# Expert loops with four row buffers and loads three quads ahead, unrolled by four; last combine's sum into X on VectorE

## The reference, cut to what matters

```python
x = x + _L0_ffn_ref(_layernorm(x), ...)   # 16 experts, top 2, silu(x w1) * (x w2), then w3, hidden 256
x = x + _L1_ffn_ref(_layernorm(x), ...)   # 8 experts, top 1 with a capacity, relu(x w1 + b1) w2 + b2, hidden 512
x = x + _L3_ffn_ref(_layernorm(x), ...)   # 64 x 192 tokens' attention first, then 8 experts, top 2, hidden 341
# of L3, the end:
for e in range(NE):
    hh = silu(flat @ w1[e].T) * (flat @ w3[e].T)
    out = out + weights[:, e:e+1] * (hh @ w2[e].T)
return x + out.reshape(Bx, Tx, Cx)
```

## Time and profile before

| | |
|---|---|
| median of 3 runs | 3395.41 us (3390.82 to 3404.48) |
| the profiled execution's own time | 3369.56 us |
| its span, first to last instruction | 3367.8 us |
| mean granted TensorE clock | 0.912 |
| busy: PE, DVE, ACT, POOL | 2731.9, 2195.4, 1751.4, 872.8 us |

### The profile page before, as it was taken

One profiled execution on the slowest core, in us unless ns is written; L12 is line 12 of the kernel. 1 busy time (PEld: TensorE's weight loads), 2 busy tenths in 40 slices (PEclk: granted clock), 3 DMA queues, 4 the chain that ended last, 5 costly groups with the idle time before them and its releaser, 6 DMA issues. The chain is left out here.

```text
span 3367.8 us, 68105 instructions
## 1 busy us (share of the span) xinstructions
PE 2731.9 (81%) x19770; PEld 2142.4 (64%) x19770; DVE 2195.4 (65%) x6539; ACT 1751.4 (52%) x5050; POOL 872.8 (26%) x863
## 2 busy tenths in 40 slices
PE   5799995787777686578999997899978777569995
PEld 4566674777467575366787776566655445468883
DVE  5666674444567554668888885799986677544443
ACT  2233332444466353465656563677757666445554
POOL 0222333444425333330010001000001434434331
PEclk9899997989878798889999999899999888689998
DMA  5111111222332111320000000000010000022125
GB/s 194 43 51 43 57 45 50 63 63 63 125 123 74 50 51 54 135 66 1 1 0 0 0 1 22 14 25 19 25 59 8 25 20 21 27 57 56 53 55 162
DMA packets 142570, 168.85 MB, mean 50 GB/s; under 512 B 19920, under 2 KB 118224, under 8 KB 141776
## 3 DMA queue, kind: packets, MB, share of 16 engines
q1 hardware_dynamic: 116688, 118.67, 11.9%
q0 software_dynamic: 21504, 44.74, 3.9%
q10 hardware_dynamic: 4224, 3.59, 0.4%
HBM read 115.87 MB, written 51.05 MB: 50 GB/s over the span
## 5 line engine op out<-in xcount | busy, mean ns | idle before, releaser
L1363 PE MATMUL bank<-ffn_e_xT,ffn_e_mine 128*128 128x128 f32 x3360 | 454.7, 284 | 27.3 <-ACT ffn_e_mine L1297 11.7
L1221 POOL DMA_INDIRECT y_rows<-ffn_e_rows_out,ffn_e_scatter_at x352 | 339.1, 963 | 522.4 <-DVE ffn_e_rows_out L1249 331.1
L1363 PEld LDWEIGHTS bank<-ffn_e_xT,ffn_e_mine 128*128 128x128 f32 x3360 | 421.8, 199 | 35.4 <-issue 30.0
L744 POOL DMA_INDIRECT sorted_rows<-ffn_rows,ffn_slot x320 | 315.9, 987 | 229.7 <-issue 218.3
L1269 DVE TENSOR_TENSOR ffn_e_hid<-ffn_e_act,bank 128x256 f32<-128x256 f32 (+1 forms) x280 | 135.9, 485 | 274.1 <-ACT ffn_e_act L1323 214.8
L1373 PE MATMUL bank<-ffn_e_mine,ffn_e_hid 128*128 128x128 f32 x1968 | 292.0, 283 | 9.0 <-issue 5.0
L1297 ACT ACTIVATE ffn_e_mine<-constants 128x512 f32 (+1 forms) x352 | 250.4, 712 | 93.3 <-issue 80.6
L1373 PEld LDWEIGHTS bank<-ffn_e_mine,ffn_e_hid 128*128 128x128 f32 x1968 | 258.1, 197 | 15.3 <-issue 6.6
L2736 ACT ACTIVATE gnn_prob<-bank,gnn_low 128x256 f32<-128x256 f32 x512 | 203.1, 500 | 108.0 <-DVE gnn_low L2650 108.0
L1323 ACT ACTIVATE ffn_e_act<-bank 128x256 f32<-128x256 f32 (+1 forms) x280 | 120.5, 430 | 244.1 <-PE bank L1363 199.3
L1257 DVE TENSOR_SCALAR ffn_e_mine<-constants 128x256 f32 (+2 forms) x352 | 124.0, 354 | 131.1 <-PE bank L1373 68.1
(11 more groups left out here) (514 smaller groups left out, 6558.3 us busy)
## 6 DMA issues: line engine op xcount, KB each, us to landing
g_adj<-in_adjT SPq DMA_DIRECT2D x48, 512.0 KB, 3.8
ffn_e_rows_in<-sorted_rows SPq DMA_DIRECT2D x346, 66.0 KB
ffn_c_y<-y_rows SPq DMA_DIRECT2D x80, 256.0 KB, 3.1
g_adj_rows<-in_adj SPq DMA_DIRECT2D x16, 512.0 KB
gnn_adj<-in_adjT SPq DMA_DIRECT2D x16, 512.0 KB, 3.9
constants<-in_ffn SPq DMA_DIRECT2D x1, 6281.0 KB, 23.0
y_rows<-ffn_e_rows_out,ffn_e_scatter_at POOLq DMA_INDIRECT x352
constants<-in_ffn SPq DMA_DIRECT2D x1, 5204.0 KB, 15.4
```

What stands on the lines that cost most here:

```text
L744: eng.indirect_dma_start(c.sorted_rows, bass.IndirectOffsetOnAxis(r.slot[par][:, k, j:j + 1], 0), r.rows[par][:, j, :], None).then_inc(r.d ...
L1221: g.indirect_dma_start(c.y_rows, bass.IndirectOffsetOnAxis(scatter_at[par][:, k:k + 1], 0), rows_out[par][:, k, :], None).then_inc(scatter ...
L1363: ins = pe.matmul(chunk(part, ch), chunk(weights[:, i * HALF:(i + 1) * HALF], ch), x, start=True, stop=True)
```

## The change

In `moe_experts`, `rows_in` has four buffers for two, and the semaphores of their loads four for two. The load of quad q waits for the transposes and the token columns of quad q-4 where it waited for those of quad q-2. The loops of SP, DVE, ACT and PE go through a new `by_fours`: four quads written out, a loop whose body is four quads (7, 3 and 7 times round), and the last two or four quads written out. POOL's loop stays.

In the last `moe_combine` alone, PE does nothing and ACT's copies back to `X` are gone. DVE, after its weighed sum of a turn, waits for it and adds it to `X`, and counts up `rows_ready`. SP waits for that alone.

```diff
+def by_fours(eng, body, count=TURNS):
+    stop = 4 + 4 * ((count - 5) // 4)
+    for t in range(4):
+        body(t, t, t == 0, False)
+    with eng.Fori(4, stop - 3, 4) as t:
+        for i in range(4):
+            body(t + i, i, False, False)
+    for t in range(stop, count):
+        body(t, t % 4, False, t == count - 1)
...
-        rows_in = [sb(f"rows_in{i}", [P, Q, ROW]) for i in range(2)]
+        rows_in = [sb(f"rows_in{i}", [P, Q, ROW]) for i in range(4)]
...
-                    wait_past(sp, xT_ps, q - 1)
-                    wait_past(sp, token_ready, q - 1)
+                    wait_past(sp, xT_ps, q - 3)
+                    wait_past(sp, token_ready, q - 3)
                     for k, at in zip(mine, places):
-                        sp.dma_start(rows_in[par][:, k, :], c.sorted_rows[ds(at, P), :]).then_inc(gathered[par], 16)
-                every_turn(sp, load, QUADS)
+                        sp.dma_start(rows_in[four][:, k, :], c.sorted_rows[ds(at, P), :]).then_inc(gathered[four], 16)
+                by_fours(sp, load, QUADS)
...
-                every_turn(v, quad, QUADS)
+                by_fours(v, quad, QUADS)
...
-                every_turn(a, quad, QUADS)
+                by_fours(a, lambda q, four, first, last: quad(q, four % 2, first, last), QUADS)
...
-                    pe.wait_ge(gathered[par], 8 * Q * (q - par) + 16 * Q)
+                    pe.wait_ge(gathered[four], 4 * Q * (q - four) + 16 * Q)
...
-                every_turn(pe, quad, QUADS)
+                by_fours(pe, quad, QUADS)
...
                     if t >= DEEP:
-                        sp.wait_ge(added_ps, t - DEEP + 1)
+                        sp.wait_ge(rows_ready if ends else added_ps, t - DEEP + 1)
                         if ends:
-                            sp.wait_ge(rows_ready, t - DEEP + 1)
                             store(t - DEEP)
...
                         ins.then_inc(summed, 1)
+                        if ends:
+                            v.wait_ge(summed, t + 1)
+                            rows_ = c.X[:, ds(t * TT, TT), :]
+                            v.tensor_tensor(rows_, rows_, acc[:], ALU.add).then_inc(rows_ready, 1)
...
-                for t in range(TURNS):
+                for t in range(0 if ends else TURNS):
                     par, bank = t % DEEP, B[t % 8][:]
...
-                    if t >= 2:
+                    if t >= 2 and not ends:
                         rows_out(t - 2)
-                rows_out(TURNS - 2)
-                rows_out(TURNS - 1)
+                for t in range(TURNS if ends else TURNS - 2, TURNS):
+                    rows_out(t)
```

More of the change, by code:

```diff
@@ L1165, in moe_experts @@
             "first_copied second_copied other_ready token_ready targets_set xT_ps xT_ready h_ps act_ready hid_ready y_ps y_ready").split())
-        gathered, scattered = ([c.dma_sem[name, n, i] for i in range(2)] for n in ("gathered", "scattered"))
+        gathered, scattered = ([c.dma_sem[name, n, i] for i in range(count)] for n, count in (("gathered", 4), ("scattered", 2)))
         def first_banks(k):
@@ L1200, in _, with load @@
             def _(sp):
-                def load(q, par, first, last):
+                def load(q, four, first, last):
                     mine = range(Q // 2) if first else range(Q)
@@ L1228, in _, with set_targets @@
             def _(v):
-                def set_targets(q, par):
-                    v.wait_ge(gathered[par], 8 * Q * (q - par) + 16 * Q)
+                def set_targets(q, four):
+                    v.wait_ge(gathered[four], 4 * Q * (q - four) + 16 * Q)
                     at = ds(q * Q, Q)
                     now = counted(v, q + 1)
-                    v.tensor_tensor(other[:], rows_in[par][:, :, D + 1], r.tile_order[:, at], ALU.not_equal).then_inc(other_ready, 1)
+                    v.tensor_tensor(other[:], rows_in[four][:, :, D + 1], r.tile_order[:, at], ALU.not_equal).then_inc(other_ready, 1)
                     v.wait_ge(other_ready, now)
-                    v.scalar_tensor_tensor(other[:], other[:], float(TOKENS), rows_in[par][:, :, D], ALU.mult, ALU.add).then_inc(token_ready, 1)
+                    v.scalar_tensor_tensor(other[:], other[:], float(TOKENS), rows_in[four][:, :, D], ALU.mult, ALU.add).then_inc(token_ready, 1)
                     v.wait_ge(token_ready, now)
@@ L1258, in copy_second, with quad @@
                                     ALU.mult).then_inc(second_copied, 1)
-                def quad(q, par, first, last):
+                def quad(q, four, first, last):
                     experts = quad_experts(v, q)
@@ L1278, in quad @@
                         if k == 0:
-                            set_targets(q, par)
+                            set_targets(q, four)
                         if k == 3 and not first:
-                            results(q - 1, 1 - par)
+                            results(q - 1, (four + 1) % 2)
                 for k, e in zip(range(AHEAD), quad_experts(v, 0)):
                     copy_second(k, e)
-                every_turn(v, quad, QUADS)
+                by_fours(v, quad, QUADS)
                 results(QUADS - 1, 1)
@@ L1376, in _, with quad @@
                 to_features(0, 0)
-                def quad(q, par, first, last):
+                def quad(q, four, first, last):
+                    par = four % 2
                     for k in range(Q):
@@ L1381, in quad @@
                         if k == 0 and not last:
-                            to_features(q + 1, 1 - par)
+                            to_features(q + 1, (four + 1) % 4)
                         if not (first and k < LAG):
                             second_product(*unit_before(q, par, k, LAG))
-                every_turn(pe, quad, QUADS)
+                by_fours(pe, quad, QUADS)
                 for k in range(LAG):
@@ L3384, in program @@
         c.bank = [ctx.enter_context(nc.psum_tensor(f"bank{i}", [P, 512], F32)) for i in range(8)]
-        c.dma_sem = {(name, n, i): c.sem(f"{name}_{n}{i}") for name in MOE for n in ("dispatched", "gathered", "scattered", "padded") for i in range({"padded": 1, "dispatched": 4}.get(n, 2))}
+        c.dma_sem = {(name, n, i): c.sem(f"{name}_{n}{i}") for name in MOE for n in ("dispatched", "gathered", "scattered", "padded") for i in range({"padded": 1, "scattered": 2}.get(n, 4))}
         c.w_ready = {n: c.sem("w_ready_" + n) for n in order}
```

4 lines of the change are left out of this document (2 added, 2 removed).

## The result

The changed kernel takes 3369.51 us (median of 4 runs, 3366.19 to 3378.20), the kernel before beside it 3399.05 us (4 runs, 3390.82 to 3404.48): a ratio of 0.9921, 95% interval 0.9901 to 0.9941. That is 29.5 us or 0.8% faster, about half of the 63 us that were forecast. The time lies in the range, which reached up to the rival in which the queue takes the gain back. So the two spans can't be subtracted. Stage by stage, the trace after is 11 us longer in the first graph layer, 5 us longer in the attention (neither is touched by the change), and 10.0 us shorter in the last combine.

The account below looks back on a forecast made before the run. PE was taken as the bound (81% busy), waiting for rows in ffn0, with SP's issuing next. Savings of 44 + 1 + 12 + 0 + 6 = 63 us from 3395.4 gave 3332 us, range 3288 to 3380.

Parts of the forecast that it names:

- the queue takes the gain back: Rival: bursts meet all four scatters, SP needs 8.0 us a quad in ffn0; 22 us saved, 3373 us, chance 0.15.
- rows 7: Profile rows in ffn0: first product through at 624.34, ACT's silu only at 627.52, when the load burst ends.
- Rows earlier, ffn0: Loads further ahead in ffn0 cut a quad from 8.51 to 7.1 us, saving 44 us; bounds 77 and 10.
- held completions: PE's completions reaching others late during a burst beside scatters; priced in ffn0 at mean 0.5 us a quad.
- SP's pace: SP's issuing in ffn0, 6.92 us a quad without waits, taken as 7.1, would set the stage's pace.
- ffn1: 18.8 us of row waits go, a third of 1.45 us a quad returns; 12 us saved, bounds 20 and 3.
- ffn3: Rows earlier in ffn3: no row wait to remove, bursts fall on the same work; 0, bounds -10 and +10 us.
- Loops by four: Jumps back 17 times in place of 38 on SP, DVE, ACT and PE; 0 us, bad-side bound 43 us.
- The last combine: Sum moved to DVE, transfers bind at 2.62 us a turn from 2.93; 6 us saved, bounds 2 and 10.
- rows 12: Profile rows of the last combine: DMA engines in use 0.90 of the time at 270 GB/s.
- PE's pace in `ffn0`: Rival: shorter bursts, SP needs about 5.2 us a quad, PE sets 6.02; 102 us saved, 3293 us, chance 0.14.
- The slower case: Rival: bursts meeting four scatters grow 1.4 us; ffn3 loses 43 us over 31 quads; 3427 us, chance 0.06.

Follow-up runs that it names:

- second held set: Set of single executions in which PE's completions reached other engines late; the unchanged kernel before took 3360.18 us in it.
- lead2: Changed kernel with loads released two quads ahead in place of three, four buffers kept; 3338.62 us, one execution.
- after_again: The changed kernel, unaltered, run again in a set where completions were not late; 3074.36 us, 0.9926 of the kernel before.
- before_third: The kernel before, unaltered, profiled again in a set where completions were late; 3360.18 us, one execution.

## Why the prediction was right or wrong

*What bounds the kernel.* The rows were read rightly: PE waited for rows, its clock fell behind the waits, and SP was behind DVE. Wrong was the reading of rows 7. "PE's completions reach the others late during a burst beside scatters" named the burst as the cause. The long burst and the late silu were two effects of the scatters: after the change they fell apart (bursts of 2 us, silu 3.7 us late between them), with one scatter in `ffn3` the hold went while the loads stayed, and in the attention there is a hold without any load.

*Rows earlier, ffn0: the step that failed.* 44 us were forecast (8.51 to 7.1 us a quad), and the first two traces show 2 us (8.44), those of the second held set 6 (8.45 to 8.26 in `lead2`). The step that failed is the price of the "held completions": a mean of 0.5 us a quad with the clock at full level, where PE's waits measured 45.0/31 = 1.45 and the clock fell. (The wait for rows went from 53.4 us to 0; the forecast had left some 0.9 us of it in every quad, behind SP.) I had let them return in every other quad and expected the lag of two units (2.2 us) to hide the rest. In fact the median lateness rose from 1.42 to 2.33 us once PE no longer stood waiting for rows, which fits a wait for rows and a hold that lay side by side before. And the clock did not come back: I "keep the clock at full level", it is 0.93, and PE is busy 216.15 us where the sum had 186.6. By idle time alone a quad would be 6.02 + 1.45 = 7.5 us; the other 0.95 is PE busy for longer, (216.15 - 186.6)/31. The slow clock explains about 0.6 of it: a granted clock of 0.93 is 0.07 x 261.5 = 18 us lost (the 24 us read from the trace before are 0.08 x 263.9 = 21 in this way). The rest, 11 us of the stretch, is not explained by a row; stops between matrix instructions that are too short to count as idle would look like this.

SP's pace was misread as well. It never bound PE, which waits for no row. But it isn't 6.92 us either: by the forecast's own formula SP takes (261.5 - 8.6)/31 = 8.16 us a quad after the change, though its bursts are short, because its register reads stretch while the scatters run. In `after_again`, not held, the same formula gives (179.7 - 18.6)/31 = 5.20. So SP's time without its semaphore waits was not what SP needs; part of it was the hold.

*ffn1.* 12 us forecast, at 13 quads (125.50 for 128.30) 3 us measured, the lower bound, with 7 for the same count in the second held set (0.51 us a quad). More than "a third" came back: 17.6 us of waits under DVE and issue where 18.8 for rows had been.

*ffn3.* 0 forecast, 0.09 us a quad longer measured (3 us over its 34 quads), inside the bound of 10 us. Right, and rightly named as the stage where the hold shows bare.

*Loops by four.* 0 forecast, 6.5 us measured where nothing is held, not located. The trace after has a handful of instruction packets in `ffn0`'s loop (6 between 620 and 850 us, for 1 in the earlier trace rows) and no idle time beside them. The Trainium skill, page "Runtime: NRT & Kernel Launch", section "Instruction fetch mechanics", has a taken branch out of the engine's two pages stall for a fetch; if all of the 6.5 us were such stalls, each of the 17 jumps would cost 0.4 us, and no row shows even that.

*The last combine.* 6 forecast, 10.0 measured in the first two traces, 10.8 and 11.8 in the others. The mechanism was right: neither chain binds and the transfers do. The term mis-sized is their rate. I took 300 GB/s, 2.62 us a turn; they run at 352 to 360, 2.2 a turn, since the 0.90 of share and 270 GB/s in rows 12 were, as it turned out, a stage still held back in part by its chain. 0.4 us in each of 12 turns is the missing 5 us.

*The rivals.* "The queue takes the gain back" came nearest in size, 22 us for 29.5, and its mark, "PE's idle time would stand under ACT and DVE", is what the trace shows. It also has SP at 8.0 us a quad (8.16). Its mechanism is not what the trace shows: the bursts became shorter, not longer, and PE didn't wait for SP. PE's pace in `ffn0` (6.02 us a quad) did come, at 5.80, with SP at the 5.2 us that the rival gave it, but only where nothing is held. The slower case, held completions that grow, has its beginning in the lateness of 2.33 us, yet `ffn3` did not grow by it. (Its 43 us count 31 quads, where `ffn3` has 34: 48 us.)

*The signs.* No waits for rows in `ffn1`, `ffn3` at 9.7 us a quad, SP's waits for DVE gone in `ffn0` (8.6 us) and still there in `ffn3` (80.0), and a DMA share above 0.95 in the combine came. A wait for rows of 0.9 us in every quad, 7.1 us a quad and a clock above 0.97 did not. And the bursts of 1.9 us, which were to show PE's pace, came with 8.44 us a quad: a sign taken from the wrong cause.

*What stays open.* The medians give 29.5 us (interval 20 to 34). The combine accounts for 10 to 11 and the expert stages of the second held set (`lead2` against `before_third`) for 12; the first two traces show nothing of the latter, and its first graph layer alone differs by 11 us between executions, so I can't place the rest. Nor is it known what makes the condition: of six sets of runs two were held (before at 3360 to 3399 us) and four not (3100 to 3105), with the same packet times. The record gives the same chip number for the second held set and for two that were not held, so if the number names one chip, it isn't a fixed property of the chip. That the late loads of the held kernel were an effect of the scatters rests on the comparison of sets (53.4 and 45.1 us of waits for rows in the held ones, 9.5 in another), not on a run that removed the scatters in `ffn0`. By what way scatters delay a signal, no run shows.

## What to carry to other kernels

When a wait and a late signal stand in the same quad, ask first whether one cause makes both; removing the wait then only uncovers the signal, and the sum has to be made with the whole lateness against the slack (3.7 against 2.2 us here), and with the slow clock beside the gaps that remain. An engine's time without its waits is what it needs only if nothing stretches its own instructions (SP's came out at 6.92 us before, 8.16 after, and 5.20 not held). Two suspects that always stand side by side in a stretch (the loads' burst and the scatters) are not told apart by it; the forecast should carry a case for each, and a run, or another stage of the same trace, that has only one of them decides. And where a stage's transfers share its time with a chain, their rate in it (270 GB/s here) need not be the ceiling of the stage without the chain (360).

## What the runs showed of the hardware

In two of six sets of runs, signals came late beside GpSimd's indirect DMAs. With four in a row, 0.96 us each and one in 1.26 us, TensorE's completion reached ScalarE 3.7 us after the product's end in the quad shown (the median silu of `ffn0` was 2.33 us late), and some of SyncE's register instructions took 0.7 us each meanwhile. With one in place of four the delay was gone in `ffn3` (0 of 136 silus over 1.5 us late, for 55), and 408.1 us of attention with indirect DMAs and no plain ones took 323.8 in another set. In the other four sets the delay did not occur, with the same program, and the kernel before was 8 to 9% faster; 31 quads of its `ffn0` took 262 to 264 us held and 193.9 not held. A gap of 1.45 us a quad went with a granted clock of 0.93 in `ffn0`, yet in `ffn1` of `lead2` 19.3 us in 13 quads, 1.48 each, went with 1.00, so the mean gap alone doesn't tell the clock. Two streams of loads and one of stores together reached 360 GB/s.
